# A two-pass normalise-and-scale kernel: VectorE's first-half rows written out with fixed addresses, and each row's last spread moved to GpSimd

## The chip, the cores and the metric

One core of one Trainium2 chip runs the kernel. The metric is the device time of one execution in microseconds, the median of several. The profiled execution has a time and a span of its own.

## The reference

The input x has shape 2 x 512 x 256 x 256 (batch, channel, height, width) in float32. It is normalised in 32 groups of 16 channels. Of the normalised x two depthwise sums are made for each channel and batch element, one over the height (weights w1, giving 256 values along the width) and one over the width (weights w2, giving 256 values along the height):

```
xl1 = bn_relu(dwconv(x, w1))      # column sums
xl2 = bn_relu(dwconv(x, w2))      # row sums
dot_cb = einsum('bck,bck->cb', xl1, xl2)
num = dot_cb.reshape(b, c)        # (512, 2) read as (2, 512)
num = softmax((num @ lw1.T + lb1) @ lw2.T + lb2)
out = x + group_norm(x) * num[:, :, None, None]
```

Because the (channel, batch) table of dot products is read row by row, the first 256 channels of both batch elements (16 groups) fill the first row of `num`, which scales batch element 0; the last 256 channels fill the second row, which scales batch element 1.

## The kernel before

x is read in 128 half-units of 2 MB: 64 units `u` (a group is two units, `2g` and `2g+1`) times two batch elements `b`. A half-unit lies in a slot of `xs`, 128 partitions by `JH` = 16 rows by 256 columns. The program runs through three stages.

First half (`u` below `FIRST` = 32, both `b`): SyncE loads each half-unit (line 344) into a slot after `free_of_statistics` (lines 325 to 328) has seen that VectorE, ScalarE, GpSimd and TensorE are through with what lay there. Five units of batch element 0 (`KEPT`) stay in their slots. For each half-unit
- ScalarE squares it with a running sum (line 867);
- TensorE makes the column sums (lines 644 and, for group 15, 634);
- VectorE makes the row sums of 13 (`DVE_ROWS`) of the 16 rows, one instruction for a row (line 1077: product with the filter in PSUM, summed into one column of `y2s`), in four sets of 4, 4, 4 and 1 rows, each of which raises `rows_done`;
- GpSimd multiplies the other 3 rows (line 464) and adds them in three halvings (lines 470, 474, 480), in `tree_unit(u)`, for both `b` of a unit together. VectorE sums the 32 columns left in `finish_rows(u)` (line 1121), which raises `y2_done`.

When a group's row sums are complete, `spread_rows` (line 307) multiplies them with a mask into one of two buffers `y2m[:, k % 2]`, and TensorE's `turn_rows(k)` (line 681, two matmul instructions for a group) brings them into `ps_y2`. A spread `k` first waits until `y2_turned` shows that turn `k - 2` has left its buffer free. In the first half the spreads 0 to 14 are GpSimd's (`spread_early`), with 12 and 13 after `tree_unit(30)` and 14 after `tree_unit(31)`. Spread 15 is VectorE's (`spread_late`), after `finish_rows(31)`. On TensorE the turns 12 and 13 stand ahead of the convolution of unit 31, and the turns 14 and 15 in `finish_row(0)`, which ends with `keep_warm(6)` (line 762) and `add_logits` (line 755).

Turn of the first row: `last_quad(0)` on VectorE (group moments, then statistics of `ps_y1` and `ps_y2` at line 1176, and a string of small operations, two of which wait for powers made on GpSimd), `softmax(0)`, and `coefs_ready`. From there the kept units are scaled (lines 1245 and 947) and stored.

Second half (units 32 to 63): batch element 0 is scaled and stored as it is read (`scale_first`), the first half's units are read again and scaled (`rework`), and the row sums of groups 16 to 31 are VectorE's, with help of GpSimd; all their spreads are VectorE's, the last, 31, ahead of `last_quad(1)`. After the second softmax batch element 1 is scaled: six half-units lie in their slots, all others are read again (line 403), scaled (line 1245) and stored. Loads are SyncE's queue, nearly all stores ScalarE's (line 952).

```
for u in range(FIRST):          # VectorE
    for b in range(B):
        multiply_rows(u, b)
        if b == 0 and u:
            finish_rows(u - 1)
...
finish_rows(FIRST - 1)
spread_late(FG - 1)
last_quad(0)
softmax(0)
```

Of the kernel before, what the change touches and what calls it, by code (L numbers as in the profile page):

```python
# [5 lines left out]
B, C, H, W = 2, 512, 256, 256  # L6
G = 32
# [19 lines left out]
DVE_ROWS = JH - POOL_ROWS  # L27
# [87 lines left out]
def conv_preact(nc, x, w1, w2, g1, b1, g2, b2, w2_rows, lw1, lb1, lw2, lb2, out):  # L115
# [9 lines left out]
    with ExitStack() as ctx:  # L125
# [155 lines left out]
        def batch_of(g, b):  # L281
            return g // QG if g < FG else FQ + g - FG + max(0, g - SPLIT) + (b if g >= SPLIT else 0)
# [125 lines left out]
        def _(pool):  # L408
# [71 lines left out]
                    nc.gpsimd.tensor_tensor(tree[:, u % 2, b], prod[:, b, :, 0:32], prod[:, b, :, 32:64],  # L480
                                            ALU.add).then_inc(tree_done, 1)

            def spread_early(k):
                if k == 0:
                    pool.wait_ge(masks_summed, 1)
                pool.wait_ge(y2_done, 2 * (k + 1))
                spread_rows(nc.gpsimd, k).then_inc(y2_spread[0], 1)

            def group_factors(k):
# [62 lines left out]
                    pool.sem_inc(masks_built, 1)  # L552

            for u in range(FIRST):
                tree_unit(u)
                setup(u)
                if u % 2 == 0 and u:
                    g = u // 2 + 1
                    pool.wait_ge(pe_read_x, 2 * (g - 1))
                    build(g)  # L560
                for q in range(FQ - 1):
                    if 2 * u in (stage(q, 16), stage(q, 18)):
                        k = QG * q + 2 * u - stage(q, 16)
                        spread_early(k)
                        spread_early(k + 1)
                    if 2 * u == stage(q, 20):
                        group_factors(q)
                    if 2 * u == stage(q, 24):
                        channel_factors(q)
                if u == FIRST - 2:  # L570
                    spread_early(FG - 4)
                    spread_early(FG - 3)
            spread_early(FG - 2)
            group_factors(FQ - 1)

            def multiply_late(u):
# [14 lines left out]
            for g in range(FG, G):  # L591
                if g == FG:
                    pool.wait_ge(coefs_ready, 1)
                if g + 1 < G:
                    pool.wait_ge(pe_read_x, filters_before(2 * g - 1, 1))
                    build(g + 1)
                if g in PROD_GROUPS:
                    multiply_late(2 * g)
                if g > SPLIT:
                    group_factors(batch_of(g - 1, 1))  # L600
                if g in PROD_GROUPS:
                    multiply_late(2 * g + 1)
                if g % QG == 2 and g // QG - 1 >= FQ:
                    channel_factors(g // QG - 1)
                group_factors(batch_of(g, 0))
            group_factors(batch_of(G - 1, 1))

        @block.tensor
        def _(pe):
# [62 lines left out]

            def turn_rows(k):
                q, a = k // QG, k % QG
                if k < FG - 1:
                    pe.wait_ge(y2_spread[0], k + 1)
                else:
                    pe.wait_ge(y2_spread[1], k + 2 - FG)
                if q and a == 0:
                    pe.wait_ge(dots_ready, 2 * q)  # L680
                nc.tensor.matmul(ps_y2[32 * a:32 * a + 32, :], own2[:, q % 2], y2m[:, k % 2],
                                 start=True, stop=True).then_inc(y2_turned, 1)
# [349 lines left out]
        def _(dve):  # L1032
# [28 lines left out]
            def multiply_rows(u, b):  # L1061
# [14 lines left out]
                def row(out, x_row, total):  # L1076
                    return nc.vector.scalar_tensor_tensor(  # L1077
                        out=out, in0=x_row, scalar=1.0, in1=ps_w2[g % 2][:, 0:W],
                        op0=ALU.mult, op1=ALU.mult, accum_out=total)

                def set_of_rows(i, junk):
                    x_set, total_set = xs[:, s, bass.ds(i * (SET * W), SET * W)], sums[:, bass.ds(i * SET, SET)]
                    for j in range(SET):
                        last = row(junk[:, j, :], x_set[:, j * W:(j + 1) * W], total_set[:, j:j + 1])
                    last.then_inc(rows_done, 1)

                if u < FIRST:
                    with dve.Fori(0, SETS - 1) as i:
                        dve.wait_ge(rows_done, i + (before - SETS + 1))
                        set_of_rows(i, early_junk[:, bass.ds(i * SET, SET), :])  # L1090
                    dve.wait_ge(rows_done, before)
                    j = DVE_ROWS - 1
                    row(early_junk[:, j, :], xs[:, s, j * W:(j + 1) * W], sums[:, j:j + 1]).then_inc(rows_done, 1)
                elif b == 0 and g in PROD_GROUPS:
                    for c in range(CHUNKS):
                        dve.wait_ge(chunk_made, chunks_before(g) + CHUNKS * (u % 2) + c + 1)
# [25 lines left out]
                                        AX.X, ALU.add).then_inc(y2_done, 1)  # L1122

            def spread_late(k):
                if k < FG:
                    dve.wait_ge(y2_done, 2 * (k + 1))
                else:
                    dve.wait_ge(rows_done, SETS * (4 * (k + 1) + 1))
                spread_rows(nc.vector, k).then_inc(y2_spread[1], 1)

            def group_moments(k):
# [140 lines left out]
                        if 2 * u + b == stage(q, 28):  # L1272
                            dot_products(q)
            finish_rows(FIRST - 1)
            spread_late(FG - 1)
            last_quad(0)
            softmax(0)
            dve.wait_ge(rstd_ready, FQ)
# [8 lines left out]
            for u, b in SEQUENCE[2 * FIRST:]:  # L1287
# [21 lines left out]
                    spread_late(G - 3)  # L1309
                if position(u, b) == stage(Q - 2, 30):  # L1310
                    spread_late(G - 2)
            spread_late(G - 1)
            last_quad(1)
            softmax(1)
            dve.wait_ge(rstd_ready, batch_of(G - 1, 1) + 1)
# [40 lines left out]
```

## Time and profile before

| | us |
|---|---|
| median of 3 runs | 1702.09 |
| lowest and highest | 1701.56, 1702.25 |
| the profiled execution | 1700.61 |
| its span | 1698.9 |

| engine | busy us | share | instructions |
|---|---|---|---|
| TensorE matmul | 488.8 | 29% | 2872 |
| VectorE | 1035.7 | 61% | 2733 |
| ScalarE | 656.7 | 39% | 510 |
| GpSimd | 535.6 | 32% | 493 |
| DMA | 721.65 MB | 424 GB/s over the span | |

Busy time is summed over instructions that moved data; waits and register work are not in it. The page cuts the span into 40 slices of 42.5 us. The first half ends in slice 8, counted from 0, and the second at the start of slice 26. A bandwidth below its neighbours' shows where the DMA engines ran dry. In timelines a row is the start in us, the time in us, engine and line, and in brackets the idle time ahead of it with what ended it; where several instructions are merged (x2), the time runs from the first start to the last end.

### The profile page before, as it was taken

Reading aid. Unit: us, or ns where it says so; the run is one execution under the profiler, and the core shown is the slowest. Engines: PE = TensorE matmul, PEld = TensorE weight load, DVE = VectorE, ACT = ScalarE, POOL = GpSimd, SP = SyncE. Lnnn points to the kernel's source line nnn. Section 1 sums busy time; section 2 is a strip of 40 time slices with the busy share of each in tenths; the row PEclk is TensorE's granted clock in tenths of the full one; section 3 lists DMA queues with packets and bytes.
Section 4 is the critical chain, followed back from the end, with each engine's and each line's share of the span. In section 5 each row is a group of like instructions: output and inputs, shape, how many; then the busy total and the mean of one; then the engine's idle time right before and its main releaser. Section 6 shows DMA issues by size and latency. Waiting matters only on the chain.

```text
span 1698.9 us, 13361 instructions
## 1 busy us (share of the span) xinstructions
PE 488.8 (29%) x2872; PEld 166.0 (10%) x2872; DVE 1035.7 (61%) x2733; ACT 656.7 (39%) x510; POOL 535.6 (32%) x493
## 2 busy tenths in 40 slices
PE   3588766660333321323233254420000000000000
PEld 1122212220010100000001022200000000000000
DVE  5899999988667586676857688782222222222220
ACT  4688887864544454545535547500000000000000
POOL 7689888840335444452335010000000000000000
PEclk8899987885666665666667576665555555555555
DMA  9999999989999999999999999999999999999999
GB/s 392 425 427 427 426 427 428 426 336 420 431 431 431 428 430 431 432 431 431 431 430 431 431 431 429 428 392 432 431 431 431 432 431 430 431 432 431 432 431 405
DMA packets 51979, 721.65 MB, mean 425 GB/s; under 512 B 6225, under 2 KB 6737, under 8 KB 8018
## 3 DMA queue, kind: packets, MB, share of 16 engines
q1 hardware_dynamic: 33922, 458.84, 63.6%
q10 hardware_dynamic: 18000, 262.15, 36.1%
q8 instruction: 23, 0.38, 0.1%
q14 instruction: 34, 0.28, 0.0%
HBM read 452.53 MB, written 268.44 MB: 424 GB/s over the span
## 4 chain that ended last, share of the span: by engine, by line
DMA 31%; another core or an unknown queue 26%; DVE 10%; issue 4%; POOL 3%; PE 3%; ACT 2%; SPq 1%; DVEq 1%; ACTq 0%; POOLq 0%
DMA xs<-in_x 23%; DMA out<-xs 8%; DVE xs L1245 3%; DVE xs L1103 2%; POOL xs L587 2%; PE ps_part L644 2%; DVE y2s L1106 2%; ACT xs L947 1%; DVE filters L1077 1%; SPq L403 1%; ACT sq_junk L867 1%; PE ps_part L762 0%; DVEq L1077 0%; DVE xs L1077 0%
## 5 line engine op out<-in xcount | busy, mean ns | idle before, releaser
L867 ACT ACTIVATE sq_junk<-xs 128x4096 fp8e5<-128x4096 f32 x128 | 463.1, 3618 | 198.4 <-DMA xs<-in_x 190.3
L1245 DVE TENSOR_SCALAR xs<-xs,scale,shift 128x4096 f32<-128x4096 f32 x91 | 223.5, 2477 | 354.3 <-DMA xs<-in_x 353.7
L644 PE MATMUL ps_part<-xs,filters 128*32 128x512 f32 x1792 | 286.2, 795 | 516.3 <-DMA xs<-in_x 507.3
L1077 DVE SCALAR_TENSOR_TENSOR xs<-xs,ps_w 128x256 f32 (+1 forms) x832 | 294.2, 416 | 29.0 <-DMA xs<-in_x 18.8
L587 POOL TENSOR_TENSOR xs<-xs,filters 128x2048 f32<-128x2048 f32 x40 | 180.5, 4543 | 90.7 <-ACT filters L881 90.7
L947 ACT ACTIVATE xs<-xs,shift,scale 128x4096 f32<-128x4096 f32 x32 | 121.5, 3798 | 164.9 <-DVE xs L1245 128.7
L644 PEld LDWEIGHTS ps_part<-xs,filters 128*32 128x32 f32 x1792 | 78.5, 139 | 709.2 <-issue 709.2
L1103 DVE TENSOR_TENSOR xs<-xs,ps_w 128x4096 f32<-128x4096 f32 x26 | 114.7, 4412 | 52.4 <-PE ps_part L644 49.7
L507 POOL TENSOR_TENSOR factors_b<-var,minus_half 128x2 f32<-128x2 f32 (+1 forms) x19 | 12.4, 651 | 394.6 <-DVE var L1142 394.6
L1097 DVE TENSOR_REDUCE y2s<-xs 128x8 f32<-128x2048 f32 x40 | 91.2, 2284 | 68.6 <-POOL xs L587 68.6
L464 POOL TENSOR_TENSOR xs<-xs 128x768 f32<-128x768 f32 x64 | 116.2, 1825 | 44.8 <-DMA xs<-in_x 41.8
L1077 DVE SCALAR_TENSOR_TENSOR filters<-xs,ps_w 128x256 uint8<-128x256 f32 x288 | 103.7, 417 | 24.3 <-DVE filters L1077 14.1
L1106 DVE TENSOR_REDUCE y2s<-xs 128x16 f32<-128x4096 f32 x26 | 114.9, 4420 | 2.7
L1077 DVE DVE_READ_ACCUMULATOR xs<-xs,ps_w (+1 forms) x832 | 68.5, 82 | 0.0
L470 POOL TENSOR_TENSOR xs<-xs 128x384 f32<-128x384 f32 x64 | 63.0, 1006 | 0.0
L659 PE MATMUL ps_part<-xs,filters 128*32 128x256 f32 x384 | 35.3, 534 | 35.9 <-DMA xs<-in_x 35.9
L434 POOL TENSOR_TENSOR filters<-own,filters 128x512 f32<-128x512 f32 x32 | 37.8, 1181 | 0.9 <-PE ps_part L659 0.7
L474 POOL TENSOR_TENSOR xs<-xs 128x192 f32<-128x192 f32 x64 | 36.7, 595 | 0.0
L889 ACT ACTIVATE y_part<-ps_part 128x256 f32<-128x256 f32 x58 | 21.6, 380 | 27.1 <-PE ps_part L644 15.1
L670 PE MATMUL ps_y<-y_part,fold 128*32 128x512 f32 x64 | 31.4, 622 | 0.0
L1245 DVE TENSOR_SCALAR filters<-filters,scale,shift 128x4096 f32<-128x4096 f32 x5 | 12.1, 2410 | 29.2 <-DMA filters<-in_x 29.2
L733 PE MATMUL ps_l<-xs 128*128 128x512 f32 x64 | 29.6, 605 | 0.0
(143 smaller groups left out, 521.6 us busy)
## 6 DMA issues: line engine op xcount, KB each, us to landing
xs<-in_x SPq DMA_DIRECT2D x208, 2048.0 KB, 24.1
out<-xs ACTq DMA_DIRECT2D x120, 2048.0 KB, 26.9
filters<-in_x SPq DMA_DIRECT2D x5, 2048.0 KB, 18.2
out<-filters ACTq DMA_DIRECT2D x5, 2048.0 KB, 86.3
out<-xs SPq DMA_DIRECT2D x3, 2048.0 KB, 15.8
xs<-in_lw SPq DMA_DIRECT2D x2, 2048.0 KB, 16.4
filters<-in_w_rows SPq DMA_DIRECT2D x1, 512.0 KB, 3.9
filters<-in_w SPq DMA_DIRECT2D x1, 512.0 KB, 9.1
```

Of the source, the lines that this page charges most:

```text
L434: nc.gpsimd.tensor_tensor(taps[:, g % 2, :, CG * qp:CG * (qp + 1)], own[:].unsqueeze(1).to_broadcast([P, JR, CG]), bc(w1_sb[:, g, :], CG), ...
L464: nc.gpsimd.tensor_tensor(prod[:, b], xs[:, s, DVE_ROWS * W:].rearrange("p (r w) -> p r w", w=W), w2_copy[:, g % 2].unsqueeze(1).to_broadc ...
L470: nc.gpsimd.tensor_tensor(prod[:, b, :, 0:128], prod[:, b, :, 0:128], prod[:, b, :, 128:256], ALU.add).then_inc(added, 1)
L587: nc.gpsimd.tensor_tensor(chunk(c), x_rows[:, c * CHUNK_ROWS:(c + 1) * CHUNK_ROWS], w2_late[:].unsqueeze(1).to_broadcast([P, CHUNK_ROWS, W ...
L644: last = nc.tensor.matmul(ps_part[g % 2][32 * a:32 * a + 32, :], taps[:, g % 2, hf * JH + j, :], xs[:, s[0]:s[1] + 1:s[1] - s[0], j * W:(j ...
L867: nc.scalar.activation(sq_junk[:], xs[:, s, :], ACT.Square, accum_out=sq_sum[:, u % 2, u // 2, b:b + 1], saturate=False).then_inc(squared, 1)
L947: nc.scalar.activation(xs[:, s, :], xs[:, s, :], ACT.Identity, scale=scale[:, 0, g:g + 1], bias=shift[:, 0, g:g + 1]).then_inc(done, 1)
L1077: return nc.vector.scalar_tensor_tensor(out=out, in0=x_row, scalar=1.0, in1=ps_w2[g % 2][:, 0:W], op0=ALU.mult, op1=ALU.mult, accum_out=total)
L1097: nc.vector.tensor_reduce(sums[:, c * CHUNK_ROWS:(c + 1) * CHUNK_ROWS], chunk(c), AX.X, ALU.add).then_inc(rows_done, SETS // CHUNKS)
L1103: nc.vector.tensor_tensor(x_rows, x_rows, ps_w2[g % 2][:, 0:W].unsqueeze(1).to_broadcast([P, JH, W]), ALU.mult).then_inc(products_done, 1)
L1106: nc.vector.tensor_reduce(sums, x_rows, AX.X, ALU.add).then_inc(rows_done, SETS)
L1245: return nc.vector.tensor_scalar(buffer(s), buffer(s), scale[:, b, g:g + 1], shift[:, b, g:g + 1], ALU.mult, ALU.add)
```

## The change

VectorE: for the first half's half-units the hardware loop over three sets of four rows (with addresses and the awaited value of `rows_done` in registers) and the thirteenth row behind it become 13 instructions with constant addresses, in the same four sets with the same waits and increments.

Spreads: `spread_early` becomes `spread_on_pool`, which can also wait for the second half's rows. GpSimd takes spread 15 (behind `tree_unit(31)`, where 14 stood) and spread 31 (ahead of its last `group_factors`), both formerly VectorE's. Spread 14 moves ahead of `tree_unit(31)`. TensorE's `turn_rows` waits on the semaphore of the engine that makes each spread.

```diff
             for u in range(FIRST):
+                if u == FIRST - 1:
+                    spread_on_pool(FG - 2)
                 tree_unit(u)
...
                 if u == FIRST - 2:
-                    spread_early(FG - 4)
-                    spread_early(FG - 3)
-            spread_early(FG - 2)
+                    spread_on_pool(FG - 4)
+                    spread_on_pool(FG - 3)
+            spread_on_pool(FG - 1)
             group_factors(FQ - 1)
...
                 group_factors(batch_of(g, 0))
+            spread_on_pool(G - 1)
             group_factors(batch_of(G - 1, 1))
...
                 if u < FIRST:
-                    with dve.Fori(0, SETS - 1) as i:
-                        dve.wait_ge(rows_done, i + (before - SETS + 1))
-                        set_of_rows(i, early_junk[:, bass.ds(i * SET, SET), :])
-                    dve.wait_ge(rows_done, before)
-                    j = DVE_ROWS - 1
-                    row(early_junk[:, j, :], xs[:, s, j * W:(j + 1) * W], sums[:, j:j + 1]).then_inc(rows_done, 1)
+                    for i in range(SETS):
+                        dve.wait_ge(rows_done, before - SETS + 1 + i)
+                        for j in range(i * SET, min((i + 1) * SET, DVE_ROWS)):
+                            last = row(early_junk[:, j, :], xs[:, s, j * W:(j + 1) * W], sums[:, j:j + 1])
+                        last.then_inc(rows_done, 1)
...
             finish_rows(FIRST - 1)
-            spread_late(FG - 1)
             last_quad(0)
...
-            spread_late(G - 1)
             last_quad(1)
```

The new `spread_on_pool(k)` waits for `y2_done` at 2(k+1) if k is below 16, else for `rows_done` as `spread_late` does, and then runs `spread_rows(nc.gpsimd, k)`. `turn_rows(k)` waits for GpSimd's count at k + 1 up to 15, for VectorE's from 16 to 30, and for GpSimd's seventeenth at 31.

## Rows read from the trace of the kernel before

**Rows 1.** Page of the profile, part 2: GB/s in 40 slices of the span

```profile
GB/s 392 425 427 427 426 427 428 426 336 420 431 431 431 428 430 431 432 431 431 431 430 431 431 431 429 428 392 432 431 431 431 432 431 430 431 432 431 432 431 405
```

**Rows 2.** Windows: busy (times) PE, PEld, DVE, ACT, POOL; clock, DMA share, GB/s

```profile
75.00:330.00 255.00, 188.15 (x998) 59.07 (x998) 245.08 (x1368) 215.65 (x195) 225.38 (x265) 0.88 1.01 427
341.00:341.50 0.50, 0.50 (x1) 0.00 (x0) 0.36 (x4) 0.22 (x2) 0.50 (x1) 0.50 1.23 524
360.00:362.00 2.00, 2.00 (x24) 0.57 (x20) 1.67 (x5) 1.04 (x3) 0.00 (x0) 1.00 0.04 16
366.00:368.00 2.00, 1.35 (x10) 0.29 (x2) 2.00 (x1) 1.55 (x2) 0.24 (x1) 1.00 0.94 393
1108.00:1112.00 4.00, 4.00 (x5) 1.74 (x6) 3.02 (x21) 0.00 (x0) 1.33 (x3) 0.50 0.96 369
```

**Rows 3.** Waits of SyncE's DMA queue, 75 to 330: us in total, times, longest

```profile
SPq L328 <- PE ps_part L644: 119.9, 24, 12.3
SPq L327 <- POOL xs L464: 78.5, 23, 6.4
...
SPq L344 <- DVE xs L1077: 8.7, 14, 1.6
```

**Rows 4.** Line 344, 75 to 330: its loads from issue to landing

```profile
DMA to landing us min/median/max: 14.9/23.2/38.6
```

**Rows 5.** Waits of VectorE, 75 to 343: us in total, times, longest

```profile
DVE xs L1077 <- issue: 4.3, 14, 1.4
...
DVE xs L1077 <- DMA xs<-in_x: 0.4, 1, 0.4
```

**Rows 6.** VectorE's line 1077, its sequencer's part, 40 to 340: ns min/median/max

```profile
L1077 DVEq FUSED_REGOPS  x868: 65/93/99, 40.3 to 340.0; - x174
```

**Rows 7.** Timeline, end of the first half: start us, us, instruction, times, idle before

```profile
339.72 2.05 POOL L307 TENSOR_TENSOR y2m<-y2s,in_row 128x512 f32<-128x512 f32 x2
...
341.73 3.61 POOL L464 TENSOR_TENSOR xs<-xs 128x768 f32<-128x768 f32 x2
...
343.40 3.62 ACT L867 ACTIVATE sq_junk<-xs 128x4096 fp8e5<-128x4096 f32 x1 [2.18 <-DMA xs<-in_x]
...
348.62 0.33 SPq L344 DMA_DIRECT2D xs<-in_x  x1
...
349.08 0.35 DVE L1121 TENSOR_REDUCE y2s<-xs 128x6 f32<-128x192 f32 x1 [0.48 <-POOL xs L480]
...
349.47 1.13 DVE L307 TENSOR_TENSOR y2m<-y2s,in_row 128x512 f32<-128x512 f32 x1
...
350.56 1.14 PE L681 MATMUL ps_y<-y2m,own 128*32 128x512 f32 x3
...
351.28 1.41 DVE L1176 BATCH_NORM_STATS2 bn_st<-ps_y 128x6 f32<-128x256 f32 x4
...
351.63 5.42 PE L762 MATMUL ps_part<-mixed 128*128 128x512 f32 x12
...
357.43 1.98 PE L755 MATMUL ps_l<-mixed,dots 128*128 128x512 f32 x4 [0.39 <-DVE z L1214]
...
362.56 2.77 DVE L1245 TENSOR_SCALAR xs<-xs,scale,shift 128x4096 f32<-128x4096 f32 x1
```

**Rows 8.** Line 681 in flight 342.2 to 342.65: ns min/median/max, first, last start

```profile
L681 PE MATMUL ps_y<-y2m,own x2: 1061/1061/1061, 341.6 to 341.8; 128*32 128x512 f32 x2
```

**Rows 9.** Timeline, end of the second half

```profile
1105.31 0.69 DVE L307 TENSOR_TENSOR y2m<-y2s,in_row 128x512 f32<-128x512 f32 x1
...
1107.69 7.61 SPq L403 DMA_DIRECT2D xs<-in_x  x2
...
1107.89 7.63 PE L762 MATMUL ps_part<-mixed 128*128 128x512 f32 x12
...
1115.40 0.38 SPq L403 DMA_DIRECT2D filters<-in_x  x1
...
1123.12 11.95 ACTq L952 DMA_DIRECT2D out<-xs  x6
```

More of the change, by code:

```diff
@@ L481, in tree_unit, with spread_on_pool @@
                                             ALU.add).then_inc(tree_done, 1)
-            def spread_early(k):
+            def spread_on_pool(k):
                 if k == 0:
                     pool.wait_ge(masks_summed, 1)
-                pool.wait_ge(y2_done, 2 * (k + 1))
+                if k < FG:
+                    pool.wait_ge(y2_done, 2 * (k + 1))
+                else:
+                    pool.wait_ge(rows_done, SETS * (4 * (k + 1) + 1))
                 spread_rows(nc.gpsimd, k).then_inc(y2_spread[0], 1)
@@ L563, in _ @@
                         k = QG * q + 2 * u - stage(q, 16)
-                        spread_early(k)
-                        spread_early(k + 1)
+                        spread_on_pool(k)
+                        spread_on_pool(k + 1)
                     if 2 * u == stage(q, 20):
@@ L674, in turn_rows @@
                 q, a = k // QG, k % QG
-                if k < FG - 1:
+                if k < FG:
                     pe.wait_ge(y2_spread[0], k + 1)
+                elif k < G - 1:
+                    pe.wait_ge(y2_spread[1], k + 1 - FG)
                 else:
-                    pe.wait_ge(y2_spread[1], k + 2 - FG)
+                    pe.wait_ge(y2_spread[0], FG + 1)
                 if q and a == 0:
@@ L1124, in spread_late @@
             def spread_late(k):
[L1125 to L1128, printed above, removed]
+                dve.wait_ge(rows_done, SETS * (4 * (k + 1) + 1))
                 spread_rows(nc.vector, k).then_inc(y2_spread[1], 1)
```

## The prediction, made before the changed kernel ran

> **What bounds the kernel now.** I read the page's 40 slices first, for the DMA. They move 425 to 432 GB/s nearly everywhere; apart from the first and the last slice, only two dip clearly, to 336 in slice 8 and to 392 in slice 26 [rows 1]. Those are the turns between the halves, where a softmax has to end before anything can be scaled and stored. So the kernel is bound by its DMA traffic, and an engine sets the end only where the DMA engines run dry.
>
> The windows confirm this. From 75 to 330 us the DMA share is 1.01 at 427 GB/s, while VectorE is busy 245.08 of 255 us. At 360 the share is 0.04, and at 366 it is back at 0.94 [rows 2]. Two engines at their limit at once need a second look, so I read the waits. SyncE's queue is released mostly by TensorE (119.9 us) and GpSimd (78.5), and by VectorE for 8.7 us, 1.6 at most [rows 3]. The loads need 23.2 us at the median from issue to landing, 14.9 at least [rows 4]; 2 MB at 427 GB/s take 4.9 us, so some five loads are always outstanding (23.2 / 4.9) and at the fewest three. A load issued a little sooner then only waits longer for its share. VectorE has little slack: it waited for data 0.4 us in all [rows 5]. But it keeps pace with a DMA that is full.
>
> The timeline of the turn shows which work leaves the DMA idle [rows 7]. The last half-unit has landed when ScalarE starts on it at 343.40. GpSimd's tree of unit 31 began at 341.73 and is over when VectorE's reduction starts at 349.08, released by it. Then come VectorE's spread (349.47), TensorE's turn, statistics (351.28), the last logits (357.43) and the first scaling at 362.56; stores bring the DMA back after that. Whatever moves 362.56 moves all that follows.
>
> **The loop written out.** Removed are 868 register instructions of about 93 ns in 300 us [rows 6], most of them under the rows they serve, for what shows of them is small: VectorE is idle only 255 - 245.08 = 9.9 us in that stretch, of which 4.3 are "issue" [rows 2, 5]. The 13 row instructions and their order stay. So VectorE may gain up to 9.9 us over 52 half-units, 0.2 each, which it will spend waiting for data. Below, the value is 0; a loss would need straight code to stall, and a longest "issue" of 1.4 us [rows 5] is the nearest price, also hidden, since VectorE is done with unit 31 before GpSimd is (it is idle 0.48 us ahead of 349.08 [rows 7]). From above, if VectorE did hold the DMA back, the first half could rise from 427 to the 431 GB/s of later slices [rows 1]: 340 us x 4 / 431 = 3.2 us. I take 0, as [rows 4] show a full queue.
>
> The Trainium skill, "Runtime: NRT & Kernel Launch", section "Instruction fetch mechanics", says that taken branches break the sequential prefetch and that full unrolling is preferable. By it VectorE gains at most the 4.3 us of "issue", under the same cover; the sum stays.
>
> **Spread 14 ahead of the last tree.** GpSimd's two spreads 12 and 13 took 2.05 us, so one is 1.03 to 1.05 [rows 7]. Placed ahead of the tree it is work in front of the chain instead of behind it. It also meets a wait that it didn't have: it needs the buffer of spread 12, so turn 12 must be done. That turn could only start when spread 12 was ready, at about 340.8. Its second matmul started at 341.6 and lasted 1.06 us, to 342.7 [rows 8], since the granted clock was 0.50 there, the 1.2 GHz level [rows 2]. GpSimd, free at 341.8, would wait until 342.7, work until 343.8, and start the tree then in place of 341.73: 2.0 us late. Behind GpSimd only this tree is queued, and behind the tree VectorE's reduction. The data are there by then (343.40). From below: if turn 12's release comes sooner than its modelled end, only the 1.05 counts; from above, two matmuls of 1.06 from 340.8 one after the other, 342.9, give 2.2. I take 2.0. The tree's own length stays (341.73 to 349.08), so the reduction moves from 349.08 to 351.1.
>
> **Spread 15 on GpSimd.** VectorE's took 1.13 us, from 349.47 [rows 7], and VectorE went on to the group moments behind it. Now the reduction ends at 351.5, GpSimd's spread takes 1.05 (to 352.6), and the turn, which took 350.65 to 351.70 (the row of three matmuls at 350.56, 1.14 long), takes 352.65 to 353.7. Meanwhile VectorE makes the moments and the first two of the four statistics. Of the row at 351.28 (1.41 us for four, some 0.34 each) the third, at 351.96, is the first that needs the turn. It starts at 353.75: 1.8 us late. Of the 2.0 thus 0.2 comes back, because moments and spread now run side by side. After that all is as before: `keep_warm` from 353.6 to 359.05, 2.0 later, while VectorE's dot products release the logits at 357.43 + 1.8 = 359.2, and TensorE waited 0.39 for them before [rows 7]. The coefficients come 1.8 late.
>
> The spread of 1.13 us is itself telling: the same operation takes VectorE 0.69 at 1105.31 [rows 9], and the longer one ran beside GpSimd's spread 14. The Trainium skill, "SBUF - State Buffer", section "SBUF: two separate sides", calls the port pair that the two share an exclusive lock, which a VectorE operation with two SBUF inputs needs as well. By that rule, the trace agrees. Here it would hold one small operation of VectorE until GpSimd's spread is over at 352.6; the two statistics behind it would end at 353.3, ahead of the turn, so the rule adds nothing to the sum.
>
> **Spread 31 on GpSimd.** VectorE's was 0.69 from 1105.31; GpSimd's is 1.05, so the turn is 0.4 us late, `keep_warm` behind it too, and the coefficients at 1120.7 likewise [rows 7, 9]. The cover is DMA: SyncE's last loads ahead of the softmax were issued at 1114.97 (the second of the two from 1107.69) and 1115.40, 4 MB or 9.8 us of traffic, until 1125; the first store came at 1123.12 [rows 9]. Cover 1.8 us, need 0.4: nothing. Without cover it would be the 0.4.
>
> **Sum.** 0 + 2.0 - 0.2 + 0 = +1.8 us, as the DMA is idle until the first stores and has no slack behind them. The profiled execution is 1700.61 (span 1698.9), 1.5 under the median; it becomes 1702.4, the median 1702.09 + 1.8 = 1703.9. About 0.2%, or 3.4 us, is what a measurement of this kernel can tell from no change, so this counts as the same.
>
> **Rivals.**
> - *The clock falls before turn 15* (slower). TensorE now has nothing from about 351.1, when turn 14 is through, to 352.65. After an idle stretch from about 338.5 to 340.8 the clock stood at 0.50 from 341 [rows 2, 8]. If it falls here, `keep_warm` takes the 7.63 us that it took at the second turn, most of it at 0.50 [rows 2, 9], for 5.42 [rows 7]. Started at 353.6 it ends at 361.3, in place of 357.43 for the logits: +3.8, and up to 0.9 more when turn 15 is slow too. That gives 1705.9 to 1706.8. For it: the clock did fall in this stretch. Against: the pause is 1.5 us, not 2.3, after dense work.
> - *VectorE did hold the DMA* (faster). Place: slot release in the first half; price 3.2 us, worked out above, less 1.8: 1700.7. It decides from the point where the written-out loop brings more than 1.8. For it: VectorE waited for data only 0.4 us. Against: [rows 3, 4].
> - *Only the 1.05 counts* (the buffer is free in time): 1.05 - 0.2 = +0.85, 1702.9.
> - *The change does nothing*: the lost time comes back in later gaps of the second half (a small rework load moved, slice 9 at 420 GB/s [rows 1]), 1702.1.
>
> **How the numbers follow.** Chances: forecast 0.52, clock 0.18, VectorE held the DMA 0.08, only 1.05 0.14, nothing 0.08. The predicted time is 1703.9. The range leaves out the lowest case and most doubt below the cheap one, and takes in the clock's case: 1701.4 to 1706.8; the forecast with its bounds alone is 1702.7 to 1704.5. Slower by over 3.4 us (above 1705.5) is the clock's case and a little of the others: 0.20. Faster by as much (below 1698.7) isn't reached even by the 3.2: 0.03. Within: 0.77.
>
> **What would show it.** Right: VectorE waits for data over 5 us more in the first half, at an unchanged 427 GB/s; GpSimd waits about 1 us for turn 12 ahead of spread 14; the reduction of unit 31 starts 2.0 us later, the third statistic 1.8, the first scaling 1.8, with the DMA idle that much longer; after 1105 nothing moves the DMA. Wrong: a first half at 430 GB/s or more, a tree that isn't late, the third statistic not late, or a granted clock of 0.50 under `keep_warm` at 353.

## The result, and the profile after

| | before | after |
|---|---|---|
| median, us | 1701.87 | 1706.78 |
| runs: times, lowest to highest | 8: 1700.14 to 1702.90 | 8: 1705.70 to 1708.73 |
| the profiled execution | 1700.61 | 1706.74 |
| its span | 1698.9 | 1705.0 |

The ratio is 1.003, with a 95% interval of 1.0021 to 1.004: slower by 4.9 us of the medians. The prediction was 1703.9, so 2.9 too low; 1706.78 lies at the very top of its range (1706.8), at the place of the clock's rival. The two profiled executions differ by 6.1 us, 1.2 more, since that of before lies 1.3 below its median.

In the kernel after, line 1085 is the row of VectorE, 1128 its reduction, 689 the turns, 770 `keep_warm`, 763 the logits, 1180 the statistics and 1249 the scaling.

Page of the kernel after: GB/s in 40 slices.

```profile
GB/s 394 424 428 426 425 427 428 425 275 418 431 430 431 431 432 430 430 431 430 431 431 430 432 429 430 431 384 431 431 432 431 432 431 432 431 431 431 431 432 412
```

Against [rows 1] the first half has the same bandwidth, and slice 8 fell from 336 to 275. That accounts for the loss: 61 GB/s over a slice of 42.6 us are 2.6 MB, or 6.1 us at 427. The turn starts later and keeps the DMA waiting for longer.

Windows of after, columns as in [rows 2].

```profile
75.00:330.00 255.00, 187.38 (x1002) 59.41 (x1002) 239.12 (x1358) 213.94 (x195) 223.34 (x263) 0.87 1.01 427
...
358.00:360.00 2.00, 2.00 (x4) 0.90 (x3) 1.58 (x15) 0.00 (x0) 0.24 (x1) 0.50 0.83 319
...
366.00:368.00 2.00, 2.00 (x24) 0.65 (x20) 1.84 (x4) 0.89 (x3) 0.00 (x0) 1.00 0.06 20
```

Waits of VectorE, 75 to 343, and of SyncE's queue, 75 to 330; then the latency of the loads.

```profile
DVE xs L1085 <- DMA xs<-in_x: 13.3, 25, 1.4
DVE xs L1085 <- issue: 1.6, 1, 1.6
```

```profile
SPq L328 <- PE ps_part L650: 114.0, 22, 12.3
SPq L327 <- POOL xs L464: 83.3, 23, 7.0
...
SPq L344 <- DVE xs L1085: 5.3, 18, 0.4
```

```profile
DMA to landing us min/median/max: 14.8/23.2/38.8
```

The written-out loop did for VectorE what it says. "Issue" fell from 4.3 to 1.6 us, the wait for data rose from 0.4 to 13.3 [rows 5], and VectorE is busy 6.0 us less in the same 255 [rows 2]. Bandwidth and median latency stayed [rows 2, 4].

Timeline of after, end of the first half.

```profile
335.60 1.84 POOL L464 TENSOR_TENSOR xs<-xs 128x768 f32<-128x768 f32 x1 [3.04 <-DMA xs<-in_x]
...
342.66 2.06 POOL L307 TENSOR_TENSOR y2m<-y2s,in_row 128x512 f32<-128x512 f32 x2
...
345.26 3.62 ACT L875 ACTIVATE sq_junk<-xs 128x4096 fp8e5<-128x4096 f32 x1 [1.16 <-DMA xs<-in_x]
...
346.12 1.05 POOL L307 TENSOR_TENSOR y2m<-y2s,in_row 128x512 f32<-128x512 f32 x1 [1.40 <-PE ps_y L689]
...
347.12 3.62 POOL L464 TENSOR_TENSOR xs<-xs 128x768 f32<-128x768 f32 x2
...
354.46 0.35 DVE L1128 TENSOR_REDUCE y2s<-xs 128x6 f32<-128x192 f32 x1 [4.67 <-POOL xs L480]
...
354.89 1.05 POOL L307 TENSOR_TENSOR y2m<-y2s,in_row 128x512 f32<-128x512 f32 x1 [0.47 <-DVE y2s L1128]
...
355.42 0.53 DVE L1172 TENSOR_TENSOR own_off<-nmean,tap_sum 128x4 f32<-128x4 f32 x1
...
355.99 1.13 PE L689 MATMUL ps_y<-y2m,own 128*32 128x512 f32 x2 [2.59 <-POOL y2m L307]
...
357.05 6.98 PE L770 MATMUL ps_part<-mixed 128*128 128x512 f32 x12
357.16 0.76 DVE L1180 BATCH_NORM_STATS2 bn_st<-ps_y 128x6 f32<-128x256 f32 x2 [0.53 <-PE ps_y L689]
...
363.87 1.88 PE L763 MATMUL ps_l<-mixed,dots 128*128 128x512 f32 x4
...
368.90 8.15 DVE L1249 TENSOR_SCALAR xs<-xs,scale,shift 128x4096 f32<-128x4096 f32 x3
```

Read from below against [rows 7], the first scaling is 6.34 us late (368.90 - 362.56). The steps are these.

- The spreads 12 and 13 start at 342.66 in place of 339.72: 2.94 late. GpSimd waits for data ahead of its last work on unit 30 until 335.60, for 3.04 us. **The loads land later**, although the DMA moves 427 GB/s.
- Spread 14 waits 1.40 for turn 12 and takes 1.05. With them the tree of unit 31 starts 5.39 late (347.12 - 341.73), and the reduction 5.38.
- Spread 15 on GpSimd beside the moments gives back 0.2: the third statistic starts at 357.16, before at 351.96, so 5.2 late.
- `keep_warm` takes 6.98 us and not 5.42, at a granted clock of 0.50, which is the 1.2 GHz level, after 2.59 us without work ahead of turn 15. The logits are 6.44 late.

The second end, timeline of after:

```profile
1111.28 1.05 POOL L307 TENSOR_TENSOR y2m<-y2s,in_row 128x512 f32<-128x512 f32 x1 [14.43 <-DVE filters L1085]
...
1129.10 14.28 ACTq L960 DMA_DIRECT2D out<-xs  x7
```

Against [rows 9] the spread and the first store are 5.97 and 5.98 late, so the whole second half passes on what the first turn lost, and spread 31 adds nothing.

### The profile page after: what moved, and what is told of

It is laid out like the page before. It is cut to its first block, busy times and chain, and to the rows that moved or that the text cites. A ratio compares the mean times of both kernels' runs of the same rounds, so it can differ in the third digit from the quotient of the medians.

```text
span 1705.0 us, 11235 instructions
## 1 busy us (share of the span) xinstructions
PE 486.3 (29%) x2872; PEld 166.0 (10%) x2872; DVE 1030.0 (60%) x2731; ACT 657.0 (39%) x510; POOL 537.6 (32%) x495
## 4 chain that ended last, share of the span: by engine, by line
DMA 47%; another core or an unknown queue 26%; DVE 10%; PE 5%; issue 3%; POOL 2%; ACT 2%; SPq 1%; DVEq 0%; ACTq 0%; POOLq 0%
DMA xs<-in_x 37%; DMA out<-xs 9%; DVE xs L1249 3%; PE ps_part L650 3%; DVE xs L1085 2%; DVE xs L1110 2%; DMA xs<-in_w 1%; DVE y2s L1113 1%; ACT xs L955 1%; DVE filters L1085 1%; POOL xs L592 1%; SPq L403 1%; ACT sq_junk L875 1%; PE ps_part L770 1%
## 5 line engine op out<-in xcount | busy, mean ns | idle before, releaser
L1085 DVE SCALAR_TENSOR_TENSOR xs<-xs,ps_w 128x256 uint8<-128x256 f32 x832 | 288.8, 417 | 34.4 <-DMA xs<-in_x 31.4
L1085 DVE DVE_READ_ACCUMULATOR xs<-xs,ps_w 128x1 f32 x832 | 68.6, 82 | 0.0
```

What stands on the lines that cost most here:

```text
L1085: return nc.vector.scalar_tensor_tensor(out=out, in0=x_row, scalar=1.0, in1=ps_w2[g % 2][:, 0:W], op0=ALU.mult, op1=ALU.mult, accum_out=total)
```

## The experiments

The theories, as the expectations name them, differ over where the loss came from: from the landings (the written-out code is more code to fetch, and the fetch is DMA traffic), from the spreads, or from the clock. "q14" is the queue of instruction packets that carries most of them, 8 KB each; the packets of several engines come over it. Differences of time are against the kernel before on the same chip. "Landing" is the start of ScalarE's squaring of the last half-unit of unit 31 in the profiled execution, "q14" the queue's packets from 0 to 345 us.

"VectorE's" counts those of q14's packets that stand ahead of the landing and are VectorE's. The trace doesn't name a packet's engine, but it dates each packet, and the runs tell the two kinds apart. One kind moves when VectorE's code gets longer or shorter (e1, e9, e10) and stands where it stood when ScalarE's does (e6), and a data packet that starts as it ends takes 1.25 to 1.28 us in place of 0.61. Behind the others that data packet takes at most 1.12 us. (The last one in e5 has no data packet behind it; it stands within 0.1 us of before's last.)

| run | q14 | VectorE's | landing | first scaling | median (before) | ratio, 95% interval |
|---|---|---|---|---|---|---|
| before | 20 | 12 | 343.40 | 362.56 | | |
| after | 21 | 14 | 345.26 | 368.90 | 1706.78 (1701.87) | 1.003 (1.0021 to 1.004) |
| e1 | 22 | 14 | 345.30 | 366.28 | 1705.46 (1701.93) | 1.0017 (1.0008 to 1.0026) |
| e2 | 19 | 12 | 343.30 | 366.71 | 1704.54 (1701.93) | 1.0013 (1.0004 to 1.0023) |
| e3 | 21 | 13 | 344.21 | 374.40 | 1713.94 (1701.93) | 1.0067 (1.0053 to 1.0081) |
| e4 | 22 | 14 | 345.27 | 365.74 | 1704.26 (1701.93) | 1.0016 (1.0007 to 1.0025) |
| e5 | 20 | 12 | 343.29 | 363.18 | 1704.15 (1702.18) | 1.0011 (1.0002 to 1.002) |
| e6 | 22 | 12 | 343.37 | 363.31 | 1702.11 (1702.18) | 1.0 (0.9991 to 1.0009) |
| e7 | 21 | 14 | 345.32 | 366.97 | 1705.58 (1702.04) | 1.0022 (1.0013 to 1.0031) |
| e8 | 20 | 12 | 343.40 | 363.08 | 1701.57 (1702.18) | 0.9998 (0.9989 to 1.0006) |
| e9 | 23 | 16 | 347.66 | 366.89 | 1707.76 (1702.18) | 1.0035 (1.0022 to 1.0048) |
| e10 | 17 | 9 | 340.42 | 360.62 | 1699.25 (1702.04) | 0.9985 (0.9976 to 0.9994) |
| e11 | 21 | 11 | 342.39 | 362.73 | 1703.68 (1702.04) | 1.0008 (0.9999 to 1.0017) |
| e12 | 21 | 14 | 345.35 | 367.28 | 1705.48 (1702.04) | 1.0018 (1.0009 to 1.0028) |

**e1, the written-out loop alone.** The kernel before, with only the loop changed.

```diff
-                    with dve.Fori(0, SETS - 1) as i:
...
+                    for i in range(SETS):
+                        dve.wait_ge(rows_done, before - SETS + 1 + i)
...
```

> The loop written out, all spreads as before. Theory F (each further fetch of VectorE's instructions holds one DMA engine up, and every load then lands 0.95 us later): unit 31's last half-unit lands about 1.9 us later than in the kernel before (343.4), the first scaling starts some 2 us later (362.6 before), and the time rises by about 2 us, to a ratio of 1.001. Rival V (what counts is the order of spreads alone; the written-out loop is hidden): landing within 0.5 us of 343.4, ratio 1.000. As the prediction had it: 0.

Timeline of e1.

```profile
345.30 3.62 ACT L867 ACTIVATE sq_junk<-xs 128x4096 fp8e5<-128x4096 f32 x1 [1.22 <-DMA xs<-in_x]
...
345.86 5.42 PE L634 MATMUL ps_part<-xs,filters 128*32 128x256 f32 x58
...
351.99 0.35 DVE L1120 TENSOR_REDUCE y2s<-xs 128x6 f32<-128x192 f32 x1 [2.16 <-POOL xs L480]
```

No spread was moved, and the last landing is 1.9 late as in after; that of the half-unit before the last two is 2.95 late (335.52 for 332.57), and the reduction, which follows from it over GpSimd, 2.9. The time is 3.5 longer. So the landings belong to the loop. The first scaling is 3.7 late, as 0.8 more comes behind the reduction: the convolution of unit 31 ran at a mean granted clock of 0.57 from 342 to 350, and VectorE waited 0.39 for TensorE's sums behind it before it could go on with the moments.

**e2, the spreads alone.** The kernel after, with the loop of before.

```diff
-                    for i in range(SETS):
...
+                    with dve.Fori(0, SETS - 1) as i:
...
```

> The three spreads moved, the loop kept. Theory F: landing as before, 343.4 within 0.5 us, as the program of VectorE is not longer. The tree starts 2.45 us late (1.4 of waiting for turn 12 and 1.05 of spread 14), the third statistic 2.2 late, and keep_warm at the lower clock adds about 1: first scaling at 362.6 + 3.3, time +3.3 us. Rival V': the landing shift of the changed kernel comes from the moved spreads: landing 345.3 here too, and time +5.

Timeline of e2.

```profile
342.67 1.05 POOL L307 TENSOR_TENSOR y2m<-y2s,in_row 128x512 f32<-128x512 f32 x1 [1.01 <-PE ps_y L689]
343.68 3.62 POOL L464 TENSOR_TENSOR xs<-xs 128x768 f32<-128x768 f32 x2
...
352.55 1.92 PE L689 MATMUL ps_y<-y2m,own 128*32 128x512 f32 x2 [2.48 <-POOL y2m L307]
354.39 7.45 PE L770 MATMUL ps_part<-mixed 128*128 128x512 f32 x12
```

The landing is that of before. GpSimd waits 1.01 for turn 12 and the tree is 1.95 late: here the prediction's 2.0 stands almost to the digit. What follows is its clock rival in full: TensorE waits 2.48, turn 15 takes 1.92 in place of 1.05 (350.65 to 351.70, worked out in the prediction), `keep_warm` 7.45. The first scaling is 4.15 late, the time 2.6 longer.

**e3, the loop kept, with 256 more instructions in VectorE's code.** Four increments of a semaphore that nobody reads, ahead of each half-unit's rows.

```diff
+                    for _ in range(4):
+                        dve.sem_inc(padding, 1)
                     with dve.Fori(0, SETS - 1) as i:
```

> The kernel before with four increments of an unused semaphore ahead of each first-half half-unit on VectorE: 256 instructions more, the loop kept. Theory F: about as many instructions more as the written-out loop brings, so two fetches more by 343 and landing about 1.9 us later, first scaling 2 us later, time +2 us. Rival (the slot releases of a faster VectorE shift the landing): VectorE isn't faster here, so landing at 343.4 within 0.5 us, time +0 to +0.5 us.

The landing moved by 0.8 with one packet more, less than expected, and the time by 12.0, far more. The four cost VectorE time of their own: its rows of the first half still ran at 352, and it did not wait for data once from 75 to 343. So the looped VectorE has no slack for them, and the time doesn't tell the theories apart. The landing fits the count: 13 of VectorE's packets for 12, one more and not two; VectorE was also behind with its work. It led to e9.

**e4, after with spread 14 behind the tree again.**

```diff
-                if u == FIRST - 1:
-                    spread_on_pool(FG - 2)
...
+            spread_on_pool(FG - 2)
             spread_on_pool(FG - 1)
```

> The changed kernel with spread 14 put back behind the tree of unit 31, ahead of spread 15; all else as changed. The tree starts 2.45 us sooner than in the changed kernel; the two spreads stand one behind the other, so turn 15 comes 1.05 later than the tree alone would let it: first scaling 1.4 us sooner than in the changed kernel if the clock falls again, about 2.5 sooner if it stays. Against the kernel before: +2.5 to +3.5 us. If moving spread 14 cost nothing, the time stays at that of the changed kernel (+4.9) or rises by 1.

The landing stays late (345.27), the reduction is at 351.99 for 354.46, `keep_warm` takes 5.42 again, and the first scaling comes 3.16 earlier than in after; the median is 2.5 lower. That is what spread 14's place costs: 2.47 up to the reduction, the rest behind it, where the clock stayed. Against e1 this kernel has only the spreads 15 and 31 on GpSimd more; its first scaling is 0.5 earlier.

**e5, the next loads held back.** SyncE issues the loads of unit 32 on only when unit 31's last half-unit has landed, in the kernel before.

```diff
+            sp.wait_ge(x_loaded[slot_of(FIRST - 1, 1)], landed(slot_of(FIRST - 1, 1), ("x", FIRST - 1, 1)))
             for u, b in SEQUENCE[2 * FIRST:2 * FIRST + 4]:
                 load(u, b)
```

> The kernel before, but SyncE issues the second half's first loads only when the first half's last half-unit has landed. Theory Q (each DMA engine works its share of the loads in their order, and one engine lags because it also brings in instructions): holding back later loads cannot speed up the lagging engine, so unit 31's last half-unit lands at 343.4 as before, first scaling at 362.6 within 0.5 us, and the other engines run dry from about 332: time 0 to 5 us worse. Rival P (outstanding loads share the bandwidth, as the prediction put it): the last half-unit lands up to 10 us sooner, first scaling with it, and the time falls by 5 us or more.

Nothing was queued behind it on the DMA, and the last half-unit landed at 343.29, as in before. What this looks like in windows (PE, PEld, DVE, ACT, POOL busy; clock, DMA share, GB/s):

```profile
328.00:330.00 2.00, 0.63 (x2) 0.00 (x0) 1.98 (x13) 2.00 (x1) 1.83 (x3) 1.00 0.96 410
...
334.00:336.00 2.00, 2.00 (x28) 1.30 (x24) 2.00 (x13) 2.00 (x1) 2.00 (x3) 0.57 0.06 25
336.00:338.00 2.00, 2.00 (x34) 1.12 (x25) 2.00 (x13) 0.85 (x3) 2.00 (x5) 1.00 0.06 25
```

From 334 on the share is 0.06, which is 1/16, and 25 GB/s: fifteen of the sixteen DMA engines have finished all loads by then, and **one is some 8 us behind**. It alone decides when a half-unit has landed. The DMA view of e5, from 340.8 to 342.8, in 40 slices of 0.05 us (a packet counts in the slice in which it starts), and its packets of instructions:

```profile
GB/s 0 0 0 0 0 0 0 328 0 0 0 0 0 0 0 0 0 0 0 164 0 0 0 0 0 0 0 0 0 0 0 0 0 0 0 0 0 0 0 0
DMA packets 3, 0.02 MB, mean 12 GB/s; under 512 B 1, under 2 KB 1, under 8 KB 1
...
q14 instruction: 1, 0.01, 1.0%
```

The last 16 KB packet of data starts in the slice at 341.15 and takes 0.61 us, one of 8 KB, an instruction fetch, starts as it ends, in the slice at 341.75, and ScalarE starts at 343.29, 2.1 us after the start of the last data packet. The half-unit before had its last data packet start at 336.30 with no fetch near, and ScalarE started on it at 337.39, 1.1 after. So this fetch cost the landing about 1.0 us. Another fetch, at 339.26, changed nothing in the step of 0.6 us from one data packet to the next. It lasted 0.47 us and ran beside two data packets, at a time when only the late DMA engine had data to move, so it was on another one; it isn't one of VectorE's packets either.

**e6, ScalarE's code longer.** The kernel before, with 256 more instructions on ScalarE.

```diff
+                    for _ in range(4):
+                        act.sem_inc(padding, 1)
                     square(u, b)
```

> The kernel before with four increments of an unused semaphore ahead of each first-half squaring on ScalarE: 256 instructions more, on ScalarE. If every engine's instructions come in through the same lagging DMA engine, the last half-unit lands about 1.9 us later (345.3), as with the written-out loop. If only VectorE's (or few engines') do, it lands at 343.4 within 0.3 us and the time is within 1 us of before.

Two packets more on q14, as in e1, the landing at 343.37 and the time unchanged. VectorE's twelve stand within 0.7 us of where they stood in before, the last at 341.86; the further ones are of the other kind. So what moves the landings is not how many fetches there are but whose. TensorE's and GpSimd's code wasn't lengthened in this way.

**e7, after with three more groups of warming matmuls between the turns 14 and 15.**

```diff
                 turn_rows(QG * q + 2)
+                if row == 0:
+                    keep_warm(3)
                 turn_rows(QG * q + 3)
```

> The changed kernel with three of the warming matmuls also between turns 14 and 15 at the first row's end, where TensorE had nothing for 2.6 us. Theory K (the clock fell in that pause and made keep_warm 6.98 us long in place of 5.42, so that it, and not VectorE's products, released the logits): granted clock 1.00 until the logits, last logits 1.0 us sooner than in the changed kernel (363.9), first scaling at 367.9 in place of 368.9, time -1 us. Rival: VectorE's products were the last anyway: 368.9 and the same time.

Timeline of e7.

```profile
355.25 1.04 PE L689 MATMUL ps_y<-y2m,own 128*32 128x512 f32 x2
356.23 5.42 PE L770 MATMUL ps_part<-mixed 128*128 128x512 f32 x12
361.84 1.98 PE L763 MATMUL ps_l<-mixed,dots 128*128 128x512 f32 x4 [0.19 <-DVE z L1220]
```

`keep_warm` is back at 5.42 and the first scaling comes 1.9 earlier than in after: 0.8 of it was there already at the reduction (353.64), as GpSimd waited 0.53 and not 1.40 ahead of spread 14: turn 12 was through sooner, and the wait that ended last was that for VectorE's reduction of unit 30. The other 1.1 came behind it, with the clock. The median is 1.2 lower, and the two intervals overlap.

**e8, before with less on GpSimd ahead of the tree.** GpSimd builds group 16's taps behind the first half's work, and spread 14 stands between the two products of unit 31.

```diff
+                    if (u, b) == (FIRST - 1, 1):
+                        spread_early(FG - 2)
...
-                if u % 2 == 0 and u:
+                if u % 2 == 0 and u and u < FIRST - 2:
...
-            spread_early(FG - 2)
             group_factors(FQ - 1)
+            pool.wait_ge(pe_read_x, FIRST - 2)
+            build(FG)
```

> The kernel before with GpSimd's order at the turn changed: the taps of group 16 are built behind the last group factors in place of ahead of spreads 12 and 13, and spread 14 stands between the two products of unit 31, where GpSimd would wait for the last half-unit to land. Landing unchanged at 343.4. Spread 12 starts at 338.2 in place of 339.7, turn 12 is done by 341.5, spread 14 costs the tree nothing, and VectorE's spread 15 runs alone (0.69 in place of 1.13): first scaling 0.4 us sooner, time -0.4 us, too little to tell by the ratio. If the tree is bound by GpSimd's work and not by the landing, it moves by up to 1.6 us sooner or 1 later.

The reduction started at 349.03 for 349.08, and `keep_warm` took 6.28. The first scaling is 0.5 later, the time not told from before's.

**e9, the written-out loop with 256 more instructions.** As e1, with waits that have long been met, which took VectorE no time that would show.

```diff
                     for i in range(SETS):
                         dve.wait_ge(rows_done, before - SETS + 1 + i)
+                        for _ in range(2):
+                            dve.wait_ge(w1_loaded, 16)
```

> The written-out loop alone (spreads as before) with two waits that are already met ahead of each set of rows on VectorE: 256 instructions more than the written-out loop, which take VectorE little time. Theory F: two further fetches by 343, the last half-unit at 345.3 + 1.9 = 347.2, first scaling and time 2 us later than with the written-out loop alone: +5.5 us on the kernel before. Rival (the written-out loop shifts the landing through VectorE's timing): landing at 345.3, time as with the written-out loop alone, +3.5 us.

Waits of VectorE in e9, 75 to 343, then ScalarE's timeline and the queue q14 up to 345 us.

```profile
DVE xs L1077 <- DMA xs<-in_x: 16.7, 29, 1.3
```

```profile
347.66 3.64 ACT L867 ACTIVATE sq_junk<-xs 128x4096 fp8e5<-128x4096 f32 x1 [1.22 <-DMA xs<-in_x]
```

```profile
q14 instruction: 23, 0.19, 0.1%
```

VectorE waits more for its data than in after, so it is not what is late. The landing is 2.4 later than in e1 and 4.3 later than before, with 16 of VectorE's packets ahead of it for 14 and 12; the time is 5.6 longer than before. The first scaling is only 0.6 later than in e1, while the span is 2.9 longer. The rest arises early in the second half (a spread of VectorE is 3.8 later than e1's by 577 us: 576.6 for 572.8), and its cause stays open.

**e10, less code.** The kernel before, with a shorter loop body in the units 16 to 29.

```diff
-                        set_of_rows(i, early_junk[:, bass.ds(i * SET, SET), :])
+                        set_of_rows(i, early_junk[:, bass.ds(i * SET, SET), :], 1 if 16 <= u < FIRST - 2 else SET)
```

> The kernel before, but for units 16 to 29 the loop's body has one row in place of four, so that 9 of VectorE's 13 rows of a half-unit are left out there (the output is not the reference's), and VectorE's program is 336 instructions shorter ahead of the turn. Theory F in the other direction: 2 to 3 fetches fewer, so the last half-unit lands 1.9 to 2.9 us sooner than 343.4, at 340.5 to 341.5, with first scaling 2 to 3 us sooner and time -2 to -3 us. Rival (only VectorE's timing matters, or fetches only hurt when VectorE waits for them): landing at 343.4 within 0.3, as in the written-out loop VectorE was also ahead of time and the landing was later, not sooner.

Timeline of ScalarE in e10, and the queue q14 up to 345 us.

```profile
340.42 3.62 ACT L867 ACTIVATE sq_junk<-xs 128x4096 fp8e5<-128x4096 f32 x1 [1.22 <-DMA xs<-in_x]
```

```profile
q14 instruction: 17, 0.14, 0.1%
```

Three fetches fewer, all three VectorE's (9 for 12), the landing 2.98 us earlier, the time 2.8 shorter. VectorE also has less work here, but it had waited for data 13 to 17 us in the runs that landed late, and before's VectorE held SyncE's queue 8.7 us in all [rows 3]; the code remains as the cause.

**e11 and e12, e8 with two warming groups between the turns, and the same with the written-out loop.** Both have this edit on e8; e12 has e1's as well.

```diff
                 turn_rows(QG * q + 2)
+                if row == 0:
+                    keep_warm(2)
                 turn_rows(QG * q + 3)
```

> The kernel before with GpSimd's new order at the turn (taps of group 16 behind, spread 14 between the products of unit 31) and two warming matmuls between turns 14 and 15. With the clock kept at 1.00 the order's gain should show: first scaling at 362.1 in place of 362.6 (363.1 without the warming), time -0.5 us on the kernel before, not to be told from 0 by the ratio. If the order itself was at fault for 363.1, it stays there.

> The same as the last with VectorE's loop written out as well. Theory F: the last half-unit lands at 345.3, 1.9 us later than with the loop, and nothing else of the written-out loop costs, as the chain now hangs on the landing alone and no longer on GpSimd's work since unit 30: first scaling 1.9 us later than in the kernel with the loop, about 364.0, time +1.9 us on it. If the written-out loop costs its whole 3.7 us at the turn by itself, first scaling is at 365.8.

e11's reduction came at 348.52, but turn 15 had to stand behind the warming, and the first scaling is at 362.73: no gain, and a median 1.6 higher, at the edge of what is told from nothing. In e12 the reduction came at 351.52, and the warming matmuls, at the low clock, held turn 15 until 355.6; the first scaling at 367.28 is later than e1's. This misses its expectation and says nothing on how much of e1's loss is GpSimd's chain. No kernel that does the whole work was shown to beat the one before.

## Why the prediction was wrong

**The loop written out: 0. This step failed.** The prediction had the 868 register instructions and their cover right, and VectorE's waits for data came as named (over 5 us more: 12.9). It took a load's landing for a share of a full queue's bandwidth: "A load issued a little sooner then only waits longer for its share." Bandwidth and median latency didn't change, and the landings did, by 1.9 to 3.0 us. In e5 the last half-unit is as late with nothing queued behind it. Its landing hangs on one DMA engine of sixteen. e1, e9 and e10 show that the landings follow the length of VectorE's code (+1.9, +4.3 and -3.0 us, with 2 and 4 of VectorE's fetches more and with 3 fewer), and e6 that ScalarE's code doesn't do it. Over all runs of the table the landing moves by 0.8 to 1.1 us for each of VectorE's packets more or fewer ahead of it, and by at most 0.11 where their number is that of before. In the steady stretch the cost is seen in the landings' cadence. Timeline of ScalarE in before:

```profile
281.69 3.62 ACT L867 ACTIVATE sq_junk<-xs 128x4096 fp8e5<-128x4096 f32 x1 [0.90 <-DMA xs<-in_x]
...
286.60 3.62 ACT L867 ACTIVATE sq_junk<-xs 128x4096 fp8e5<-128x4096 f32 x1 [1.20 <-DMA xs<-in_x]
...
292.46 3.62 ACT L867 ACTIVATE sq_junk<-xs 128x4096 fp8e5<-128x4096 f32 x1 [1.43 <-DMA xs<-in_x]
...
297.35 3.62 ACT L867 ACTIVATE sq_junk<-xs 128x4096 fp8e5<-128x4096 f32 x1 [1.18 <-DMA xs<-in_x]
```

The half-units come 4.91, 5.86 and 4.89 us apart; the queue has one fetch between 286 and 288. The interval after a long one is not shorter, so the microsecond is lost for all that follows. From 218 us on there are five intervals of about 5.8 us or more in before, seven in e9 and three in e10, and each has one of VectorE's packets in it:

| | VectorE's packets at | long interval from |
|---|---|---|
| before | 234.0, 260.6, 286.7, 315.2, 341.9 | 230.8, 256.3, 286.6, 312.0, 337.5 |
| e9 | 218.6, 239.7, 258.4, 279.0, 300.8, 322.0, 339.4 | 218.5, 239.0, 254.7, 275.2, 300.7, 321.2, 336.9 |
| e10 | 220.8, 278.7, 329.1 | 220.1, 274.9, 324.9 |

The packets of the other kind (before's at 243.2 and 321.7) have none. The size of the step can be read from the packets: a fetch of VectorE's takes 0.33 us, and the data packet that starts as it ends 1.27 in place of 0.61, together 0.98. That these fetches all lie on the late engine follows from the landings, each of which comes later for them; which engine it is the trace doesn't say.

This also gives the place its part. By the time unit 30's last half-unit landed, 14 of VectorE's packets had passed in after and 11 in before, as before's twelfth came only at 341.87, at the end of the last half-unit: hence unit 30's is 3.0 late and the last landing 1.9. After and e1 are alike, as e1's one packet more on q14 comes at 344.67, behind the landing. In e11, whose VectorE runs the code of before, the twelfth came at 342.52, behind the landing, which was 1.0 us earlier. What made it come 0.65 us later than in before stays open, as does a kernel that does the whole work with less of VectorE's code, which wasn't tried.

The Trainium skill, "Runtime: NRT & Kernel Launch", section "Instruction fetch mechanics", prefers full unrolling and calls the fetch's cost mostly hidden, while it notes that the sequencer fetches over DMA queues. Here the 4.3 us of "issue" did shrink to 1.6, and the fetches cost more than that elsewhere: e1 is 3.5 us slower.

**The cover of VectorE by GpSimd.** The prediction named the landing at 343.40 and took it as fixed ("The data are there by then"). It also saw only unit 31's data. In after GpSimd is late from unit 30's last half-unit on, by 3.0, so the spreads 12 and 13 and turn 12 are late too, and the chain has no slack to take it up.

**Spread 14 ahead of the tree: 2.0.** Right in kind. In e2, with the loop as before, 1.95. In after it is 2.45 (1.40 + 1.05), 0.25 above the prediction's upper bound; in e7, where only work behind it was changed, the wait was 0.53, so this term moves by 0.9 from execution to execution with turn 12. Turn 12 ran at the low clock in after (0.54 from 343 to 345), behind 3.34 us without work, while in e7 TensorE's pause there was 1.73 and the granted clock 1.00. The rival that only the 1.05 counts is refuted by the waits of 1.01 and 1.40.

**Spread 15: -0.2.** Right: the delay fell from 5.4 to 5.2 between reduction and third statistic. The small operation held beside GpSimd's spread is there: 0.53 us for one of 0.15 before, without effect on the chain.

**The clock, chance 0.18.** The prediction counted a pause of 1.5 us. It was 2.48 in e2 and 2.59 in after. Turn 15 started in e2 where it was forecast (352.55 for 352.65), but TensorE was through with turn 14 and the work beside it at 350.07 and not at 351.1, since spread 14 had been made early. `keep_warm` took 6.98 to 7.45 us. So this rival came true together with the failed step: in e2 the logits are 4.25 late and the third statistic 2.54 (354.50 for 351.96), so the clock's part is 1.7; in after it is 1.2 (6.44 - 5.2), and e7 gave 1.1 back. The prediction had priced it at 2.0 to 2.9 above its forecast. In e1 and e4, where turn 14 stands behind the tree, `keep_warm` took 5.42. But the pause is not all of it: in e6 and e8, with no such pause ahead of turn 15, the granted clock was 0.54 and 0.57 from 350 to 352 and `keep_warm` took 5.93 and 6.28, while in before it was 1.00. So part of the 1.2 may be an execution's own; how much, one profiled execution of each kernel can't say.

**Spread 31: 0.** Right: 5.97 late there, 6.34 at the first turn.

**The sum.** Landings +3.0, spread 14 +2.4, spread 15 -0.2, clock +1.2: 6.4, against 6.34 in the trace at the first scaling. Span +6.1. That the median still lies within the range, by 0.02 us, is luck: the top of the range was the clock's case alone, and the time got there by 3.0 us of landings that the prediction had at 0 and a clock's part of about half its price. The parts alone measured 3.5 (e1) and 2.6 (e2) of the medians, together 6.1, for 4.9 in after, and their intervals cover the difference. Of the rivals, "VectorE did hold the DMA" is refuted: VectorE waited for data 13.3 us and the first half wasn't faster. "The change does nothing", by lost time that comes back in later gaps, is refuted by the 5.98 at the first store of the second end.

## What to carry to other kernels

Code is DMA traffic: where all loads are spread over the sixteen DMA engines and the kernel is bound by them, an engine's longer program can make every load land later with the total bandwidth unchanged (VectorE's did here, ScalarE's didn't), so compare the landings one by one, and the packets of the instruction queues, before a loop is written out for a few ns an iteration. Ask of anything placed ahead of a critical chain what it waits for itself. Where TensorE has a gap of some 2.5 us just before work that the end hangs on, price that work at the low clock as well.

## What the runs showed of the hardware

- One of sixteen DMA engines stood 8 us behind the others at the end of the first half (e5: share 0.06 from 334 to 342), with 427 GB/s at a share of 1.01 from 75 to 330 in before; the page of the profile shows no engine by itself.
- 256 instructions more in VectorE's straight code (e9 against e1) were two fetches of 8 KB more ahead of the landing (16 for 14) and a landing 2.4 us later; 256 more on ScalarE (e6) moved no landing.
- A fetch of VectorE's costs about 0.98 us of a DMA engine that is busy with 16 KB packets: 0.33 itself, and the data packet behind it takes 1.27 in place of 0.61 (before, at 234.0, 286.7 and 315.2).
- Loads queued behind a half-unit didn't slow its landing: with none behind it, the last one came 0.11 us earlier (e5).
- A semaphore increment that nobody waits for isn't free on an engine without slack: 256 of them, with a loop, made the kernel 12 us slower (e3); on ScalarE they cost nothing (e6).
- In the stretch of low work at the turn TensorE's clock stood at 0.50 after a pause of 2.59 us (after), and `keep_warm` took between 5.42 (before) and 7.45 us (e2); in e8 it took 6.28 without such a pause.
